# Reading the output weights, the gate and two modulation rows on ScalarE's queue, in pieces

## The reference

```python
mod = (_silu(L0_c) @ L0_wmod).reshape(L0_c.shape[0], 6, 1, -1)
sa, ca, ga, sb, cb, gb = (mod[:, 0], mod[:, 1], mod[:, 2], mod[:, 3], mod[:, 4], mod[:, 5])
ga = (2 * (ga >= 0) - 1) * jnp.maximum(jnp.abs(ga), 0.25)
gb = (2 * (gb >= 0) - 1) * jnp.maximum(jnp.abs(gb), 0.25)
h = _layernorm(x, axis=-1) * (1 + ca) + sa
x = x + ga * _L0_attn_ref(h, L0_attn_W_qkv, L0_attn_W_o)   # 16 heads of 32, rotary, causal softmax, @ W_o.T
h = _layernorm(x, axis=-1) * (1 + cb) + sb
x = x + gb * _L0_ffn_ref(h, L0_ffn_Wg, L0_ffn_balance_bias, L0_ffn_W1, L0_ffn_W2)  # top 2 of 16 experts
```

## Time and profile before

| | us |
|---|---|
| median of 3 runs | 1674.82 |
| lowest and highest of these | 1670.08, 1675.14 |
| the profiled execution, its own time | 1672.97 |
| its span (first to last instruction) | 1671.2 |
| busy in it: PE / DVE / ACT / POOL | 1420.8 / 1241.8 / 834.2 / 758.3 |
| transferred in it | 254.56 MB |

### The profile page before, as it was taken

One profiled execution on the slowest core, in us unless ns is written; L12 is line 12 of the kernel. 1 busy time (PEld: TensorE's weight loads), 2 busy tenths in 40 slices (PEclk: granted clock), 3 DMA queues, 4 the chain that ended last, 5 costly groups with the idle time before them and its releaser, 6 DMA issues. The chain is left out here.

```text
span 1671.2 us, 27857 instructions
## 1 busy us (share of the span) xinstructions
PE 1420.8 (85%) x8713; PEld 1008.6 (60%) x8713; DVE 1241.8 (74%) x2928; ACT 834.2 (50%) x1414; POOL 758.3 (45%) x675
## 2 busy tenths in 40 slices
PE   5679998899899879989988998999883999999900
PEld 3556665566566556656655565665341899999800
DVE  3577877687777768777776877788768677777778
ACT  4324647534454654345566434455523566666622
POOL 2245445342435534334544433355434677777500
PEclk9799999999999999999999999999995899999955
DMA  6544443534344463424435452433654455445389
GB/s 214 169 158 152 133 138 96 164 114 158 101 123 128 114 167 114 151 89 131 123 106 172 113 159 83 139 95 114 242 179 158 153 176 184 159 146 168 120 316 375
DMA packets 128370, 254.56 MB, mean 152 GB/s; under 512 B 15600, under 2 KB 67312, under 8 KB 127744
## 3 DMA queue, kind: packets, MB, share of 16 engines
q1 hardware_dynamic: 104192, 184.46, 35.8%
q0 software_dynamic: 13792, 47.72, 8.4%
q10 hardware_dynamic: 10272, 20.97, 3.5%
HBM read 167.34 MB, written 85.75 MB: 151 GB/s over the span
## 5 line engine op out<-in xcount | busy, mean ns | idle before, releaser
L688 ACT ACTIVATE probs<-ring 128x1024 f32<-128x1024 f32 (+3 forms) x384 | 310.3, 811 | 186.6 <-PE ring L542 117.2
L507 PE MATMUL ring<-stack_t 96*128 96x512 f32 (+3 forms) x768 | 297.7, 412 | 23.6 <-DMA stack_t<-stack_dram 13.1
L1149 POOL TENSOR_TENSOR rope_a<-rope_a,rope_b 128x256 f32<-128x256 f32 x128 | 127.7, 997 | 341.7 <-DVE rope_b L921 341.6
L485 PE MATMUL ring<-w_parts,h_hi 128*128 128x384 f32 x1024 | 273.3, 348 | 9.2 <-DVE neg_max L848 4.0
L851 DVE CUSTOM_DVE_ANT_0 ring<-ring,later_b 128x384 f32<-128x384 f32 (+3 forms) x512 | 247.1, 497 | 22.6 <-PE ring L507 21.6
L507 PEld LDWEIGHTS ring<-stack_t 96*128 96x128 f32 x768 | 143.0, 194 | 173.1 <-issue 67.8
L1135 POOL TENSOR_TENSOR prob_sum<-prob_sum,probs 128x1024 f32<-128x1024 f32 (+3 forms) x128 | 229.9, 1796 | 22.9 <-ACT probs L688 22.0
L536 PE MATMUL ring<-stack_t 128*128 128x512 f32 (+3 forms) x768 | 213.2, 360 | 22.7 <-ACT probs L688 12.4
L485 PEld LDWEIGHTS ring<-w_parts,h_hi 128*128 128x128 f32 x1024 | 189.6, 195 | 17.4 <-issue 12.3
L848 DVE TENSOR_REDUCE neg_max<-ring 128x1 f32<-128x512 f32 x256 | 175.0, 683 | 12.1 <-PE ring L507 11.1
L485 PE MATMUL ring<-w_parts,h_lo 128*128 128x384 f32 x512 | 175.9, 344 | 0.0
(11 more groups left out here) (192 smaller groups left out, 2431.9 us busy)
## 6 DMA issues: line engine op xcount, KB each, us to landing
stack_t<-stack_dram SPq DMA_DIRECT2D x384, 128.0 KB, 3.3
stack_dram<-parts SPq DMA_DIRECT2D x64, 512.0 KB, 2.6
w_parts<-w_dram SPq DMA_DIRECT2D x24, 768.0 KB, 7.7
w_sb<-y_dram SPq DMA_DIRECT2D x32, 512.0 KB, 7.0
w_sb<-w SPq DMA_DIRECT2D x22, 512.0 KB, 6.3
x_in<-x SPq DMA_DIRECT2D x32, 256.0 KB, 3.7
x<-x SPq DMA_DIRECT2D x32, 256.0 KB, 3.5
x_dram<-x SPq DMA_DIRECT2D x32, 256.0 KB, 2.9
```

The costliest lines, as they stand in the source:

```text
L485: mm = nc.tensor.matmul(ring[:, BANK[use], 0:384], lhs[:, c, cols], rhs[:, c, :], start=(k == 0), stop=(k == len(products) - 1))
L507: nc.tensor.matmul(ring[:, BANK[use], 0:width], stack_t[0:MROW, i % 2, 0, h, qt * P:qt * P + P], stack_t[0:MROW, i % 2, 1, h, kc * 512:kc ...
L688: nc.scalar.activation(probs[:, step % PROBS, :, q0:QC], ring[:, bank:bank + 2, q0:QC], ACT.Exp)\
L1149: nc.gpsimd.tensor_tensor(rope_a[:, t % 2, :], rope_a[:, t % 2, :], rope_b[:, :], ALU.add)\
```

## The change

SP's `load_mod2` is gone. ACT has two new functions. `load_w_out` issues the gate row and the first quarter of `w_out` at step 2, and one quarter more at each of the steps 3, 4 and 5; it waits for the same semaphores as `load_mod2` did. `load_mod_rows` issues the two modulation rows at step 7. POOL multiplies one quarter at a time, at steps 7, 8, 9 and 11; the first of the four waits for the gate row and for all four quarters. PE and SP wait for four gatings where they waited for two. Bytes, and elements multiplied, are the same.

```diff
-GATE_OUT = {step + 8 + n: (b, n) for step, b in LOAD_MOD2.items() for n in range(2)}
+LOAD_W_OUT = {step + 2 + n: (b, n) for step, b in LOAD_MOD2.items() for n in range(G)}
+LOAD_MOD_ROWS = {step + 7: b for step, b in LOAD_MOD2.items()}
+GATE_OUT = {step + at: (b, n) for step, b in LOAD_MOD2.items() for n, at in enumerate((7, 8, 9, 11))}
...
-                    def load_mod2(b):
...
-                        sp.dma_start(w_out[:, :, :], w_o_t).then_inc(w_out_in, 16)
-                        sp.dma_start(x1[:, 1, :], mod_dram[GA, b:b + 1, :].to_broadcast([P, D])).then_inc(gate_in, 16)
...
-                            sp.wait_ge(w_out_gated, 2 * (b + 1))
+                            sp.wait_ge(w_out_gated, G * (b + 1))
...
-                        if step in LOAD_MOD2:
-                            load_mod2(LOAD_MOD2[step])
...
-                            pe.wait_ge(w_out_gated, 2 * (b + 1))
+                            pe.wait_ge(w_out_gated, G * (b + 1))
...
+                    def load_w_out(b, g):
+                        if g == 0:
+                            if b:
+                                act.wait_ge(h2_ready, b * NT)
+                                act.wait_ge(o_ps, b * NT)
+                                act.wait_ge(x1_out, 16 * b * NT)
+                            else:
+                                act.wait_ge(mod_out, 64)
+                                act.wait_ge(w_split, G)
+                            act.dma_start(x1[:, 1, :], mod_dram[GA, b:b + 1, :].to_broadcast([P, D])).then_inc(gate_in, 16)
+                        act.dma_start(w_out[:, g, :], w_o_t[:, g, :]).then_inc(w_out_in, 16)
+
+                    def load_mod_rows(b):
+                        for k, row in ((MB_S, SB), (MB_C, CB)):
+                            act.dma_start(mod_b[:, k, :], mod_dram[row, b:b + 1, :].to_broadcast([P, D]))\
+                                .then_inc(mod2_in, 16)
...
                     def gate_out_weights(b, n):
                         if n == 0:
                             pool.wait_ge(gate_in, 16 * (b + 1))
-                            pool.wait_ge(w_out_in, 16 * (b + 1))
-                        part = w_out[:, 2 * n:2 * n + 2, :]
-                        nc.gpsimd.tensor_tensor(part, part, x1[:, 1:2, :].to_broadcast([P, 2, D]), ALU.mult)\
+                            pool.wait_ge(w_out_in, 16 * G * (b + 1))
+                        nc.gpsimd.tensor_tensor(w_out[:, n, :], w_out[:, n, :], x1[:, 1, :], ALU.mult)\
                             .then_inc(w_out_gated, 1)
```

More of the change, by code:

```diff
@@ L337, in load_x @@
                         sp.dma_start(x_in[:, u % 3, :], x_tiles[u, :, :]).then_inc(x_in_s[u % 3], 16)
-                    def load_mod2(b):
[L340 to L346, removed]
-                        sp.dma_start(w_out[:, :, :], w_o_t).then_inc(w_out_in, 16)
-                        sp.dma_start(x1[:, 1, :], mod_dram[GA, b:b + 1, :].to_broadcast([P, D])).then_inc(gate_in, 16)
-                        for k, row in ((MB_S, SB), (MB_C, CB)):
-                            sp.dma_start(mod_b[:, k, :], mod_dram[row, b:b + 1, :].to_broadcast([P, D]))\
-                                .then_inc(mod2_in, 16)
                     def load_residual(b, t):
@@ L810, in _ @@
                                 load_mod(k)
+                        if step in LOAD_W_OUT:
+                            load_w_out(*LOAD_W_OUT[step])
+                        if step in LOAD_MOD_ROWS:
+                            load_mod_rows(LOAD_MOD_ROWS[step])
                         if step in NORM_C:
```

## The result

The changed kernel takes 1676.52 us (median of 18 runs, 1668.95 to 1682.44) against 1671.42 us of the kernel before (18 runs beside them, 1663.63 to 1675.14). The ratio is 1.0032, with an interval of 1.0018 to 1.0045: about 5 us slower, where 1657 was forecast. The profiled execution has a span of 1676.2 us, against 1671.2.

The account below looks back on a forecast made before the run. Bound by DVE's wait for x in groups 3, 7 and 11, no engine being full. Terms -10.7 - 3.6 - 3.4 + 0.5 + 0 + 0.5 = -16.7 us from 1672.97 gave 1656.3, stated as 1657; range 1650 to 1668.

Parts of the forecast that it names:

- What bounds the kernel: No engine is full; in groups 3, 7 and 11 the others follow DVE's wait for x, 11.92 us in all.
- part 1: Groups 3, 7, 11: with 1.75 MB off SP's queue, x lands earlier and DVE's wait mostly goes; gain 10.7 us.
- Rival (a): Groups 3, 7, 11: the load of x stays as late, since the bytes are the same; 1670.6 us, chance 0.11.
- Part 2: Groups 3, 7, 11: PE's clock mostly doesn't fall after the waits; gain 3.6 us, ends 0 and 5.0.
- Part 3: Groups 3, 7, 11, step 9: quarter gatings on POOL shorten DVE's 16-column instruction and PE's wait; gain 3.4 us.
- Part 4: Seven more issues on ACT in each of four groups, mostly beside a running ACTIVATE; cost 0.5 us, bounds 0 and 12.0.
- What is late next: Groups 3, 7, 11: claimed nothing takes the wait's place, as PE reaches x_hat's transposition just when ACT delivers it.
- clock windows of 0.5 that merely move: Listed sign of a wrong forecast: PE's slow-clock windows shift elsewhere instead of staying at 1.0 through steps 6 and 7.
- Part 5: Step 7: POOL's wait for all quarters is covered by idle time before the rope sum of step 8; 0 us.
- Part 6: Group 15: denominators come earlier, but the output projection needs the quarter behind POOL's sum; +0.5 us, between -1 and +3.
- a gating at step 7 that starts more than 5 us after POOL came to it: Listed sign of a wrong forecast: POOL's first gating held up by more than 5 us.
- Rival (c): Gating comes late as POOL waits at step 7 for recently issued quarters; slower than before, 1681 us, chance 0.03.

Follow-up runs that it names:

- e4: Kernel before with SP's loads of w_out, gate and modulation rows five steps earlier, gating still in halves; 1653.47 us, ratio 0.9891.
- e8: Kernel before with the same SP loads moved to step 3, behind the load of x on SP's queue; 1654.63 us, ratio 0.9907.
- e1: Changed kernel with both modulation rows issued by ACT at step -5 instead of step 7; 1660.84 us, ratio 0.9941.
- e9: Kernel before with SP's load_mod2 five steps earlier and gating in quarters at steps 7, 8, 9 and 11; 1648.81 us, one run.
- e5: Kernel before with only the gating changed, to quarters at steps 7, 8, 9 and 11; 1671.15 us, ratio 0.9996.
- e2: Changed kernel with group 15's gate row and w_out quarters issued at steps -6 to -3, ahead of the expert weights; 1669.65 us, ratio 0.9982.
- e7: Changed kernel with the two modulation row reads replaced by two tiles of x, same bytes from 128 different rows; 1669.55 us, ratio 0.9998.
- e10: Changed kernel with one modulation row issued at step -5 and the other left at step 7; 1660.92 us, one run.
- e3: Changed kernel with both modulation rows at step -5 and group 15's gate and quarters at steps -6 to -3; 1653.45 us, ratio 0.9899.

## Why the prediction was wrong

**What bounds the kernel** and **part 1** were right. The wait for x was the one to take away, and it went, even in group 7, where 1.2 us were expected to stay. Landing was estimated at 314.1 to 315.1 in group 3; it came at 303.77 + 6.9 = 310.7, with room to spare; the rate of 0.24 MB per us was too low, which cost the forecast only those 1.2 us. Rival (a), that the load of x stays as late, didn't come.

**Part 2** was right in kind, too small, and not right in what would last. e4, e8 and e1 have the clock at 1.00 where it had fallen, and parts 1 and 2 together gave 17.3 us (e4) against 14.3. With the 11.9 us of the waits taken off, 5.4 are left for part 2, where 3.6 were forecast and 5.0 was the end; the cap of 1.65 us a group, read from one row of DVE's slack, didn't hold in groups 3 and 11 (2.0 and 1.9). But in the changed kernel the clock fell again four steps later.

**Part 3** was right in groups 3, 7 and 11 when tried without ACT's loads (3.1 us in e9, 5.0 in e5, 3.4 forecast, with 0 to 4.3 as ends). In the changed kernel itself the 16-column instruction took 0.18 us and met no gating, because the new wait had moved it.

**Part 4 is the first step that failed.** It priced the two modulation rows as issue time on ACT, 0.1 us a group. The issues were indeed small: 0.33 to 0.46 us each in group 3, beside the running ACTIVATE, with at most 0.2 us of idle time before ACT's next instruction. What it left out is the 0.5 MB behind them. Part 1 counted every byte that stood ahead of x on either queue, but no part counted what stood ahead of, or beside, the next loads on SP's queue, the six of `stack_t`. They weren't in the rows read, because before the change PE didn't wait for them. This step cost 15.4 us in three groups (after against e1; 12.2 with e2's profile of the same groups), and it nearly cancels parts 1 to 3. "What is late next" was asked only for the chain that the removed wait had delayed, and not for what the moved transfers would now meet. The last of the listed signs, "clock windows of 0.5 that merely move", came true by it.

**Part 5** was right. POOL waited 0.60 us for the quarters in group 3 and nothing followed.

**Part 6 is the second.** It gave +0.5 us, from -1 to +3; measured were +10.0 in the profile of the changed kernel, and +7.3 to +7.8 in e1, e7 and e10. The issues were placed well (4.9 to 9.9 us into the group forecast, 4.2 to 9.2 measured). The rate was not: 1.25 MB were to take 6 to 9 us at a half to a third of 404 GB/s, and they took from 1168.2 to 1173.5 + 10.2 = 1183.7, 15.5 us, about a fifth of that rate. They came in behind and beside the expert weights, which had been issued first. Undoing that brings 5 to 6 us (e2, e3). The sign "a gating at step 7 that starts more than 5 us after POOL came to it" came true here, at 7.58 us. The place of the fourth quarter was reasoned rightly as far as PE's start goes: with early loads PE starts the projection 22.8 us into the group in e5 and 21.8 in e9, 22.9 before. What part 6 left out is the clock behind PE's wait: the projection takes 6.04 us in e5 and 5.40 in e3, where it starts at 22.2, but 3.70 in e9, whose group 15 lasts 93.8 us like e4's. In the changed kernel PE starts 4.8 us later than before, and the projection takes 3.05 us more; the remaining 2 us were not taken apart. Rival (c), the late gating, was therefore true in group 15, where it was priced at 7 us; it was given a chance of 0.03, since I set it against the cover in the other groups. In group 15 POOL had 4.70 us of idle time before its sum of step 10, which a wait of 7.58 us used up. Even so, (c) alone wouldn't have turned the sign: 1657 + 9.5 would still have been faster than before. The rows at step 7 did that.

The range ended at 1668 because no rival held a new wait of PE for a `stack_t` load. e1 and e3 show how near the rest was: without the rows at step 7 the kernel takes 1660.84 us, and with early quarters in group 15 as well 1653.45.

## What to carry to other kernels

When transfers are moved to another queue, list the loads of every queue that are in flight with them at their new place (here the rows took 4 to 7 us to land in groups 3, 7 and 11, the quarters up to 10 in group 15), with how late each may land, and not only those that they used to stand ahead of. First try the other order on the same queue: here it gave the gain of parts 1 and 2 (e8, 0.9907) with no new wait. Price a new wait of TensorE together with the clock behind it: of the 15.4 us lost, 8.4 were waiting.

## What the hardware showed that was not expected

- Two transfers of 256 KB issued by ACT in the middle of six loads of SP (128 KB each) went with the slowest of them at 7.6 us instead of 3.5, with the DMA engines at a share of 0.92 and 0.80 over windows of 4 us; in single microseconds from 320 to 327 the share lies between 0.74 and 1.11, so they are full in some of them. With half the bytes the slowest took 4.5 to 5.4 us, against 6.1 to 7.6 (e10, single run).
- Issuing from ACT cost little in group 3: 0.33 to 0.46 us on its queue, beside a running ACTIVATE, at most 0.2 us of idle time behind it.
- Under a queue full of expert weights (318 to 411 GB/s in all, by windows of 4 us from 1168 to 1184), `w_out` quarters of 256 KB from a second queue landed 9.6 to 10.2 us after their issue, and 1.25 MB of them got a fifth of the rate.
- PE's waits for `stack_t` of 0.5 to 1.4 us left its clock at 1.00 (e7, e10). All eight of 2.0 to 3.5 us (after, e2, e7) came with a clock at its lower level, for 3 us in three of them and for 7 us in the others.
- POOL's fourth quarter and a DVE sum of 1024 columns lengthen each other by order of start: DVE first, 1.90 and 2.25 us (e5); POOL first, 1.27 us for POOL and 1.97 for DVE (e9), where they take 1.26 and 1.23 us elsewhere.
- One memory row spread over 128 partitions may disturb others somewhat more than 128 rows of the same bytes: the slowest `stack_t` loads took 6.1 to 7.6 us (after, e2) against 5.3 to 6.2 (e7). The time ratios, 1.0032 and 0.9998, differ too, but group 15 makes a part of that.
